# Which queue issues the loads of queries and residual tokens in the fused attention and routing stage

## The chip, the core and the metric

The kernel runs on one core of a Trainium2 chip. A core has TensorE (PE, matmuls), VectorE (DVE), ScalarE (ACT), GpSimd (POOL) and SyncE (SP), each with its own instruction stream, and 16 DMA engines that move data between SBUF and HBM. SyncE and ScalarE each have a hardware queue for DMAs (q1 and q10 in the trace), GpSimd a software queue (q0). The streams meet at semaphores. The metric is the device time of one execution in microseconds, lower is better.

## The reference

For x of 4 sequences of 2048 tokens with 512 channels the reference computes one layer:

```
x = x + layernorm(attention(layernorm(x)))          # linear attention with random features, 16 heads of 32
x = x + layernorm(ffn(layernorm(x)))                # 32 experts, top 4 of each token, plus a shared expert

attention: q_phi, k_phi = sorf_phi(rope(q)), sorf_phi(rope(k))      # exp of 128 features a head
           S, sum_k = sum over l of k_phi v,  sum over l of k_phi
           out = (q_phi S) / max(q_phi sum_k, EPS)                  # numerator over denominator, for each head and token
           return out @ w_out.T
```

The denominator is one number for a head and a token. It is what travels through DRAM below.

## The kernel before

The 8192 tokens are cut into NG = 16 groups of G = 512, each into A = 4 tiles of 128. A first stage normalises x, stores it centred (`xc`), projects it to queries, keys and values and stores the queries (`qk`, `norm`); a second sums the keys' features. The stage of this case is the third, `attend_and_route_programs` (line 782). Five programs, one for each engine, run over STEPS steps; in step s each engine does its part for several tiles at different distances behind, written out by hand. `group_at(s, lag)` says which group, if any, is due in step s with that lag. After the stage the same engines go on with the expert stage.

In step s TensorE makes the logits of quarter s+1 of the queries (L891, a quarter is 4 heads of a group), the numerators and denominators of quarter s (L901, L910), projects tile s-8 (L922), and turns and gates an earlier tile (L934, L948). ScalarE makes the features from the logits (`make_phi`, L991, twice a step, and the logits' place is free for TensorE only then), squares, copies the numerators to `heads` (L999), copies turned tiles (L1030) and makes the high half of normalised tiles (L1021). VectorE adds, measures and makes the low halves, and chooses experts.

Once a group, the denominators make a round trip. With n the group:

- VectorE, step 4(n+1): `read_total` (L1109) writes `den`.
- SyncE: `spread_share(n)` (from L855) stores it with four DMAs (L860), waits, loads it back with 64 tokens on each of 128 partitions as `dens` (L862).
- VectorE, step 4(n+1)+1: `make_share` (L1116) inverts it.
- SyncE stores `share` (L864), waits, and loads it with four broadcast DMAs into `spread`, 1 MB in SBUF (L869).
- VectorE, step 4n+6: `divide` (L1121), `heads` times `spread`. Its next instructions stand behind it. ScalarE, in the same step, waits for it in `make_at_high` (L1005), then goes on; VectorE makes the low half (L1125), and TensorE can project the group.

SyncE's queue carries, besides, the loads of a group's queries (`load_q`, by `load_heads`, lines 79 to 86: three DMAs of 512 KB and one of 32 KB, L82 and L84), into two buffers of which one is `keep["ahead"]`, and of the centred tokens that are added back (`load_x`, L852, 1 MB). Its order is a loop: queries of n+1, the round trip of n-1, the tokens of n-1. ScalarE's queue carries three stores of 1 MB a group: `x1` after `make_at_high` (L1042, step 4n+14 for group n), `rows` (L1047, step 4n+16) and the turned tiles (L1052, step 4n+17). GpSimd makes the reciprocal roots and scatters slots (L1261).

Of the kernel before, what the change touches and what calls it, by code (L numbers as in the profile page):

```python
# [5 lines left out]
P = 128  # L6
# [7 lines left out]
G = 512  # L14
NG = T // G
A = G // P
EC = E // P
# [764 lines left out]
def attend_and_route_programs(nc, io, keep, t):  # L782

    with ExitStack() as tiles:
        t.ctx = tiles
        PHIS, XS = 4, 3
# [4 lines left out]
        qT = [keep["ahead"], t.sb("qT1", [KR, H, G], F16)]  # L791
# [6 lines left out]
        x = [t.sb(f"x{r}", [P, A, E]) for r in range(XS)]  # L798
# [22 lines left out]
        x_loaded, x_stored = ([t.sem(f"{n}{r}") for r in range(XS)] for n in ("x_loaded", "x_stored"))  # L821
# [16 lines left out]
        def group_at(s, lag):  # L838

            return (s - lag) // A if s >= lag and (s - lag) % A == 0 and (s - lag) // A < NG else None  # L840

        def sp_program(sp):
            def load_q(n):
                if n >= 2:
                    sp.wait_ge(logits_ready, 2 * EC * (n - 1))
                load_heads(sp, io, qT[n % 2], n, 0, q_loaded[n % 2])

            def load_x(n):
                if n >= XS:
                    sp.wait_ge(x_low_ready, A * (n - XS + 1))  # L850
                    sp.wait_ge(x_stored[n % XS], 16 * (n // XS))
                sp.dma_start(x[n % XS][:], io["xc"][n * G:(n + 1) * G, :].rearrange("(a p) e -> p a e", p=P)  # L852
                             ).then_inc(x_loaded[n % XS], 16)

            def spread_share(n):  # L855
                sp.wait_ge(den_ready, n + 1)
                if n >= 1:
                    sp.wait_ge(share_ready, n)
                for i in range(HPC):
                    sp.dma_start(io["den"][n, i], den[D * i:D * i + EC, :]).then_inc(den_stored, 16)  # L860
                sp.wait_ge(den_stored, 16 * HPC * (n + 1))
                sp.dma_start(dens[:], io["den"][n].rearrange("i c (k q) -> (i c k) q", q=KP)).then_inc(dens_loaded, 16)  # L862
                sp.wait_ge(share_ready, n + 1)
                sp.dma_start(io["share"][n].rearrange("i c (k q) -> (i c k) q", q=KP), share[:]).then_inc(share_stored, 16)  # L864
                sp.wait_ge(share_stored, 16 * (n + 1))
                if n >= 1:
                    sp.wait_ge(at_ready, n)
                for i in range(HPC):
                    sp.dma_start(spread[D * i:D * i + D].rearrange("p c n -> p (c n)"),  # L869
                                 io["share"][n, i:i + 1].rearrange("o c n -> o (c n)").to_broadcast([D, EC * G])  # L870
                                 ).then_inc(spread_loaded, 16)

            load_q(1)
            for n in range(1, NG + 1):
                if n + 1 < NG:
                    load_q(n + 1)
                spread_share(n - 1)
                load_x(n - 1)

        def pe_program(pe):  # L880
            def make_logits(q, b):
# [101 lines left out]
                    count(n)  # L983

        def act_program(act):
            def make_phi(q, b):
                m = 2 * q + b
                act.wait_ge(logits_ready, m + 1)
                if q >= 2:
                    act.wait_ge(total_ready, q - 1)  # L990
                nc.scalar.activation(phi[m % PHIS][:].rearrange("p h q -> p (h q)"), logits[:], ACT.Exp,  # L991
                                     scale=1.0 / M_SCALE).then_inc(phi_ready, 1)

            def read_numer(q):
                n, c = q // EC, q % EC
                act.wait_ge(numer_ready, q + 1)
                if n >= 2:
                    act.wait_ge(at_low_ready, n - 1)
                nc.scalar.activation(heads[n % 2][:, c, :], numer[:], ACT.Copy).then_inc(numer_read, 1)  # L999

            def make_at_high(n):
                act.wait_ge(at_ready, n + 1)
                if n >= 2:
                    act.wait_ge(y_ready, A * (n - 1))
                nc.scalar.activation(at_hl[n % 2][:, 0], heads[n % 2][:], ACT.Copy).then_inc(at_high_ready, 1)  # L1005

            def square(m):
                k = m % 2
                act.wait_ge(y_ready, m + 1)
                if m >= 2:  # L1010
                    act.wait_ge(var_ready, m - 1)
                nc.scalar.activation(squares[k][:], y[k][:], ACT.Square, scale=E ** -0.5,
                                     accum_out=mv[k][:, 0, 1:2]).then_inc(y_squared, 1)

            def make_high(m):
                n, a, k = m // A, m % A, (m + 1) % 2
                act.wait_ge(rstd_ready, m + 2)
                if a == 0 and n >= 2:
                    act.wait_ge(rows_stored[n % 2], 16 * (n // 2))
                    act.wait_ge(turned_ready, A * (n - 1))  # L1020
                nc.scalar.activation(hl[n % 2][:, a, 0, :], x[n % XS][:, a, :], ACT.Copy,  # L1021
                                     scale=rstd[k][:, 1:2]).then_inc(x_high_ready, 1)

            def copy_turned(m):
                n, a = m // A, m % A
                act.wait_ge(turned_ready, m + 1)
                if a == 0 and n >= 2:
                    act.wait_ge(gates_ready, n - 1)
                    act.wait_ge(xT_stored[n % 2], 16 * (n // 2))
                nc.scalar.activation(xT[n % 2][:, :, :, a * P:(a + 1) * P],  # L1030
                                     turned[:].bitcast(F16).rearrange("p (s c q) -> p s c q", s=2, c=EC),
                                     ACT.Copy).then_inc(xT_ready, 1)

            def make_score(n):
                act.wait_ge(gates_ready, n + 1)
                if n >= 1:
                    act.wait_ge(slots_ready, n)
                nc.scalar.activation(grown[:].rearrange("p a e -> p (a e)"), gates, ACT.Exp, scale=-1.0).then_inc(score_ready, 1)

            def store_x1(n):  # L1040
                act.wait_ge(x1_ready, A * (n + 1))
                act.dma_start(io["x1"][n * G:(n + 1) * G, :].rearrange("(a p) e -> p a e", p=P),  # L1042
                              x[n % XS][:]).then_inc(x_stored[n % XS], 16)

            def store_rows(n):
                act.wait_ge(x_low_ready, A * (n + 1))
                act.dma_start(io["rows"][n * G:(n + 1) * G, :].rearrange("(a p) n -> p a n", p=P),  # L1047
                              hl[n % 2][:].rearrange("p a s e -> p a (s e)")).then_inc(rows_stored[n % 2], 16)

            def store_turned(n):  # L1050
                act.wait_ge(xT_ready, A * (n + 1))
                act.dma_start(io["xT2"][n], xT[n % 2][:].rearrange("p s c q -> p (s c q)")).then_inc(xT_stored[n % 2], 16)  # L1052

            for b in range(2):
                make_phi(0, b)
            for s in range(STEPS):
                n = group_at(s, SCORE)
                if n is not None:
                    make_score(n)
                if s + 1 < NT:  # L1060
                    make_phi(s + 1, 0)
                if 0 <= s - SQUARE < NT:
                    square(s - SQUARE)
                if s < NT:
                    read_numer(s)
                if s + 1 < NT:
                    make_phi(s + 1, 1)
                if 0 <= s - COPY < NT:
                    copy_turned(s - COPY)
                if 0 <= s - SPLIT < NT:  # L1070
                    make_high(s - SPLIT)
                n = group_at(s, A + 2)
                if n is not None:
                    make_at_high(n)
                n = group_at(s, A - 1 + ADD + 1)
                if n is not None:
                    store_x1(n)
                n = group_at(s, A - 1 + TURN + 1)
                if n is not None:
                    store_rows(n)  # L1080
                n = group_at(s, A - 1 + COPY + 1)
                if n is not None:
                    store_turned(n)
            for k in range(2):
                act.wait_ge(xT_stored[k], 16 * NG // 2)
                act.wait_ge(rows_stored[k], 16 * NG // 2)
            for r in range(XS):
                act.wait_ge(x_stored[r], 16 * ((NG - 1 - r) // XS + 1))
# [790 lines left out]
```

## Time and profile before

| | |
|---|---|
| runs | 2131.26 us median of 3 (2128.41 to 2144.04) |
| profiled execution | 2139.98 us; 2138.2 from its first to its last instruction |
| PE busy | 1843.4 us, 86% of the span |
| DVE busy | 1183.8 us, 55% |
| ACT busy | 1071.0 us, 50% |
| POOL busy | 756.9 us, 35% |
| mean granted clock of TensorE | 0.939 of full |
| q1 (SyncE) | 239.19 MB, 38.1% of the 16 DMA engines' time |
| q10 (ScalarE) | 124.26 MB, 16.5% |
| the stage of this case | about 866 to 1410 us of the span |

A row of an engine's timeline gives the start in microseconds, the duration, the engine, the line, the operation and what it writes and reads; in brackets stands the idle time before it and what ended it. `SPq` and `ACTq` are DMA issues on SyncE's and ScalarE's queues: their duration is that of the issue, not of the transfer. A busy PE is not PE at its peak, and idle time of an engine that sets nothing costs nothing.

### The profile page before, as it was taken

To read this page: it belongs to the slowest core of one execution; us is meant where nothing else is said; L and a number is where in the kernel's file an instruction comes from. 1 tells how busy PE (TensorE), PEld (TensorE's weight loads), DVE (VectorE), ACT (ScalarE), POOL (GpSimd) and SP (SyncE) were. 2 spreads that over 40 slices of the span, in tenths; PEclk is the share of its full clock that TensorE was granted. 3 is DMA by queue.
4 is the path that set the end of the run, shared out by engine and by line. 5 is a ranking of instruction groups with operands and counts; after the bars stand their busy time and mean duration, and the time that the engine had idled before them with its cause. 6 is when DMAs were issued, how large, how long until landed. Compare 5 with 4: busy or idle time off the path is not lost.

```text
span 2138.2 us, 33516 instructions
## 1 busy us (share of the span) xinstructions
PE 1843.4 (86%) x12976; PEld 892.7 (42%) x12976; DVE 1183.8 (55%) x2055; ACT 1071.0 (50%) x1371; POOL 756.9 (35%) x716
## 2 busy tenths in 40 slices
PE   8899999999988999699789888635998999987785
PEld 6444444444436888133233333322444444443231
DVE  7676766666650000156778878762444444445786
ACT  5555554545524666566566666412444444432443
POOL 0000000000000000013578787875677777761110
PEclk9999999999998999899899999867999999998897
DMA  6636354454527888567887785443799999987983
GB/s 231 232 124 239 132 193 178 168 203 165 178 103 209 211 212 205 120 175 188 225 221 239 220 235 183 161 183 100 169 197 221 247 241 246 205 146 241 334 288 126
DMA packets 197295, 421.92 MB, mean 197 GB/s; under 512 B 34068, under 2 KB 72340, under 8 KB 180512
## 3 DMA queue, kind: packets, MB, share of 16 engines
q1 hardware_dynamic: 91632, 239.19, 38.1%
q10 hardware_dynamic: 68640, 124.26, 16.5%
q0 software_dynamic: 36864, 56.32, 14.2%
q8 instruction: 103, 1.69, 0.3%
q14 instruction: 56, 0.46, 0.1%
HBM read 237.06 MB, written 193.86 MB: 202 GB/s over the span
## 4 chain that ended last, share of the span: by engine, by line
DMA 16%; PE 11%; DVE 10%; issue 9%; POOL 7%; ACT 3%; SPq 1%; POOLq 0%; DVEq 0%; ACTq 0%
DMA acc_dram<-s_y,s_slot 6%; DMA s_spread<-share_dram 5%; POOL acc_dram L1427 3%; PE s_gates L1486 2%; PE s_y L922 2%; PE s_ups L1486 2%; POOL slot_dram L1261 2%; DMA share_dram<-s_share 2%; DVE s_heads L1121 2%; PE s_ys L1501 1%; DMA s_dens<-den_dram 1%; DMA den_dram<-s_den 1%; DVE s_stats L1652 1%; DVE s_x L1675 1%; PE s_logits L891 1%
## 5 line engine op out<-in xcount | busy, mean ns | idle before, releaser
L271 PE MATMUL s_proj<-s_xT,keep_wqkv 128*128 128x512 f16 x1536 | 343.5, 380 | 0.0
L1261 POOL DMA_INDIRECT slot_dram<-keep_filled,keep_slots x256 | 274.1, 1071 | 76.2 <-issue 73.5
L1427 POOL DMA_INDIRECT acc_dram<-s_y,s_slot x128 | 204.5, 1597 | 92.7 <-issue 36.2
L271 PEld LDWEIGHTS s_proj<-s_xT,keep_wqkv 128*128 128x128 f16 x1536 | 148.2, 98 | 184.5 <-issue 14.8
L922 PE MATMUL s_y<-keep_wo,s_at_hl 128*128 128x512 f16 x768 | 197.2, 412 | 19.2 <-DVE s_x L1133 19.0
L250 PE MATMUL s_proj<-keep_wqkv,s_xT 128*128 128x512 f16 x768 | 181.4, 395 | 32.4 <-ACT s_xT L524 32.4
L1541 ACT ACTIVATE s_gate<-s_gates 128x512 f32<-128x512 f32 x96 | 57.1, 597 | 264.6 <-PE s_ups L1486 223.6
L1611 DVE SCALAR_TENSOR_TENSOR s_h<-s_gate,s_ups 128x512 f32<-128x512 f32 x96 | 65.9, 686 | 215.0 <-ACT s_gate L1541 215.0
L542 ACT ACTIVATE s_hl<-s_rot 128x1024 f16<-128x1024 f32 x64 | 67.6, 1057 | 231.3 <-DVE s_rot L413 230.5
L991 ACT ACTIVATE s_phi<-s_logits 128x1024 f32<-128x1024 f32 x128 | 131.5, 1027 | 99.2 <-PE s_logits L891 98.4
L400 DVE TENSOR_TENSOR s_by_cos<-s_proj,s_table 128x1024 f32<-128x1024 f32 x64 | 78.3, 1224 | 185.5 <-PE s_proj L271 184.4
L352 POOL TENSOR_SCALAR s_rstd<-s_mv 128x4 f32<-128x4 f32 x16 | 3.7, 229 | 499.7 <-DVE s_mv L367 499.7
L700 ACT ACTIVATE s_phi<-s_logits 128x1024 f32<-128x1024 f32 x128 | 131.1, 1024 | 86.9 <-PE s_logits L721 86.9
L1413 POOL DMA_INDIRECT s_rows<-rows_dram,s_slot x128 | 133.1, 1040 | 42.9 <-issue 32.0
L1532 ACT ACTIVATE s_xT<-s_turned 128x1024 f16<-128x1024 f16 x128 | 125.5, 1019 | 41.4 <-PE s_turned L1463 41.4
L922 PEld LDWEIGHTS s_y<-keep_wo,s_at_hl 128*128 128x128 f16 x768 | 74.7, 104 | 161.8 <-issue 72.2
L761 PE MATMUL s_parts<-s_phi,s_v 128*33 128x128 f32 x2048 | 138.7, 278 | 3.7 <-DMA s_v<-v_dram 3.6
L1501 PE MATMUL s_ys<-s_w,s_parts 128*128 128x512 bf16 x512 | 131.0, 379 | 3.5 <-DVE s_y L1628 3.5
L1486 PE MATMUL s_gates<-s_xT,s_w 128*128 128x512 f16 x512 | 124.5, 387 | 10.3 <-ACT s_xT L1532 10.3
L250 PEld LDWEIGHTS s_proj<-keep_wqkv,s_xT 128*128 128x128 f16 x768 | 75.8, 101 | 130.8 <-ACT s_xT L524 39.6
L1486 PE MATMUL s_ups<-s_xT,s_w 128*128 128x512 f16 x512 | 121.6, 380 | 0.0
L1628 DVE TENSOR_SCALAR s_y<-s_ys,s_slot 128x512 f32<-128x512 f32 x128 | 93.9, 748 | 42.0 <-PE s_ys L1501 41.5
(166 smaller groups left out, 3154.9 us busy)
## 6 DMA issues: line engine op xcount, KB each, us to landing
qk_dram<-s_hl ACTq DMA_DIRECT2D x32, 1024.0 KB
keep_ahead<-qk_dram SPq DMA_DIRECT2D x48, 512.0 KB
acc_dram<-s_zero SPq DMA_DIRECT2D x17, 1024.0 KB, 13.1
v_dram<-s_v ACTq DMA_DIRECT2D x16, 1056.0 KB
s_v<-v_dram SPq DMA_DIRECT2D x16, 1056.0 KB
s_x<-x_in SPq DMA_DIRECT2D x16, 1024.0 KB
xc_dram<-s_x SPq DMA_DIRECT2D x16, 1024.0 KB
s_spread<-share_dram SPq DMA_DIRECT2D x64, 256.0 KB
```

The source lines that it names most:

```text
L250: mm = nc.tensor.matmul(proj[half][:, 512 * b:512 * b + 512], left, right, start=(c == 0 and i == 0), stop=(c == EC - 1 and i == 2))
L271: mm = nc.tensor.matmul(out[:, 512 * b:512 * b + 512], left, right, start=(c == 0 and i == 0), stop=(c == EC - 1 and i == 2))
L700: nc.scalar.activation(phi[n % 2][:].rearrange("p h m -> p (h m)"), logits[n % 2][:], ACT.Exp, scale=1.0 / M_SCALE).then_inc(phi_ready, 1)
L761: mm = nc.tensor.matmul(parts[ch % 2][at:at + D + 1, h // 2 * M:(h // 2 + 1) * M], v[n % 2][:, a * H + h, :], phi[half][:, h % HALF, :], s ...
L922: mm = nc.tensor.matmul(y[m % 2][:], at_hl[n % 2][:, s, c, a * P:(a + 1) * P], keep["wo"][:, w, c, :], start=(c == 0 and i == 0), stop=(c ...
L991: nc.scalar.activation(phi[m % PHIS][:].rearrange("p h q -> p (h q)"), logits[:], ACT.Exp, scale=1.0 / M_SCALE).then_inc(phi_ready, 1)
L1261: nc.gpsimd.indirect_dma_start(out=io["slot"], out_offset=bass.IndirectOffsetOnAxis(ap=slots[n % 2][:, a * K + j:a * K + j + 1], axis=0), ...
L1413: nc.gpsimd.indirect_dma_start(out=rows[r][:, a, :], out_offset=None, in_=io["rows"], in_offset=bass.IndirectOffsetOnAxis(ap=slot[e % RING ...
L1427: nc.gpsimd.indirect_dma_start(out=io["acc"], out_offset=bass.IndirectOffsetOnAxis(ap=slot[e % RING][:, a, 0:1], axis=0), in_=y[e % 2][:, ...
L1486: mm = nc.tensor.matmul(bank[:], w[:, c, i * P:(i + 1) * P], left[:, s, c, :], start=(c == 0 and s == 0), stop=(c == EC - 1 and s == 1))
L1501: mm = nc.tensor.matmul(ys[a % 2][:], parts[p % 2][:, i, s, a * P:(a + 1) * P], w[:, i, :], start=(i == 0 and s == 0), stop=(i == IC - 1 a ...
L1532: nc.scalar.activation(xT[k][:, :, :, a * P:(a + 1) * P], turned[a % 2][:].bitcast(F16).rearrange("p (s c q) -> p s c q", s=2, c=EC), ACT. ...
```

## The change

`load_q` and `load_x` move, with their waits, from SyncE's program to ScalarE's. ScalarE issues the queries of group n+2 at the end of its step 4(n+1), after `make_high` and ahead of the rows store of the same step, and the tokens of group n in step 4n+6, right after `make_at_high` and ahead of the x1 store of the same step. SyncE keeps the queries of group 1, before the loop, and the round trip of each group. Nothing of the arithmetic, the buffers or the transfers' shapes changes.

```diff
         def sp_program(sp):
-            def load_q(n):
-                if n >= 2:
-                    sp.wait_ge(logits_ready, 2 * EC * (n - 1))
-                load_heads(sp, io, qT[n % 2], n, 0, q_loaded[n % 2])
-
-            def load_x(n):
-                if n >= XS:
-                    sp.wait_ge(x_low_ready, A * (n - XS + 1))
-                    sp.wait_ge(x_stored[n % XS], 16 * (n // XS))
-                sp.dma_start(x[n % XS][:], io["xc"][n * G:(n + 1) * G, :].rearrange("(a p) e -> p a e", p=P)
-                             ).then_inc(x_loaded[n % XS], 16)
-
...
-            load_q(1)
-            for n in range(1, NG + 1):
-                if n + 1 < NG:
-                    load_q(n + 1)
-                spread_share(n - 1)
-                load_x(n - 1)
+            load_heads(sp, io, qT[1], 1, 0, q_loaded[1])
+            for n in range(NG):
+                spread_share(n)
...
         def act_program(act):
+            def load_q(n):
+                if n >= 2:
+                    act.wait_ge(logits_ready, 2 * EC * (n - 1))
+                load_heads(act, io, qT[n % 2], n, 0, q_loaded[n % 2])
+
+            def load_x(n):
+                if n >= XS:
+                    act.wait_ge(x_low_ready, A * (n - XS + 1))
+                    act.wait_ge(x_stored[n % XS], 16 * (n // XS))
+                act.dma_start(x[n % XS][:], io["xc"][n * G:(n + 1) * G, :].rearrange("(a p) e -> p a e", p=P)
+                             ).then_inc(x_loaded[n % XS], 16)
+
...
                 if 0 <= s - SPLIT < NT:
                     make_high(s - SPLIT)
+                n = group_at(s, A)
+                if n is not None and n + 2 < NG:
+                    load_q(n + 2)
                 n = group_at(s, A + 2)
                 if n is not None:
                     make_at_high(n)
+                    load_x(n)
                 n = group_at(s, A - 1 + ADD + 1)
                 if n is not None:
                     store_x1(n)
```

## Rows read from the trace of the kernel before

**Rows 1.** Busy time by stretch, nine groups: window, PE, PEld, DVE, ACT, POOL, clock, DMA, GB/s.
```profile
1061.90:1335.20 273.30, 244.97 (x1851) 90.64 (x1850) 216.79 (x497) 179.96 (x268) 210.83 (x217) 0.95 0.77 222
```
**Rows 2.** Waits of VectorE in the same stretch: us in total, times, longest.
```profile
DVE s_heads L1121 <- DMA s_spread<-share_dram: 31.3, 9, 4.1
```
**Rows 3.** Timeline of SyncE's queue, group 7: start, us, what.
```profile
1092.46 1.27 SPq L860 DMA_DIRECT2D den_dram<-s_den  x4
1095.89 0.34 SPq L862 DMA_DIRECT2D s_dens<-den_dram  x1
...
1104.78 3.32 SPq L869 DMA_DIRECT2D s_spread<-share_dram  x4
...
1111.01 1.25 SPq L82 DMA_DIRECT2D keep_ahead<-qk_dram  x3
```
**Rows 4.** Timelines of ScalarE and VectorE, group 7.
```profile
1098.04 0.37 ACTq L1047 DMA_DIRECT2D rows_dram<-s_hl  x1
...
1102.36 0.28 ACT L1038 ACTIVATE s_grown<-s_route 128x128 f32<-128x128 f32 x1 [1.52 <-issue]
...
1104.67 0.35 ACTq L1052 DMA_DIRECT2D xT_dram<-s_xT  x1
...
1116.35 0.37 ACTq L1042 DMA_DIRECT2D x_dram<-s_x  x1
...
1102.20 0.54 DVE L1116 RECIPROCAL s_share<-s_dens 128x64 f32<-128x64 f32 x1
...
1114.02 2.29 DVE L1121 TENSOR_TENSOR s_heads<-s_heads,s_spread 128x2048 f32<-128x2048 f32 x1 [3.52 <-DMA s_spread<-share_dram]
```
**Rows 5.** The rows store and the divide of group 6, timelines.
```profile
1065.26 0.37 ACTq L1047 DMA_DIRECT2D rows_dram<-s_hl  x1
...
1082.75 2.29 DVE L1121 TENSOR_TENSOR s_heads<-s_heads,s_spread 128x2048 f32<-128x2048 f32 x1 [3.33 <-DMA s_spread<-share_dram]
```
**Rows 6.** DMA queues (packets, MB, share) in 1117.5:1122.5, 1122.6:1125.6, 389.9:392.9; two issues.
```profile
q1 hardware_dynamic: 159, 1.04, 99.1%
...
q10 hardware_dynamic: 451, 0.92, 86.7%
...
q10 hardware_dynamic: 856, 0.88, 100.4%
...
383.34 1.03 ACTq L562 DMA_DIRECT2D qk_dram<-s_hl  x2
...
388.69 0.37 SPq L169 DMA_DIRECT2D s_x<-x_in  x1
```
**Rows 7.** DMA queues in 1115.8:1122.5 (queries), 1099:1102 (rows store), 1105:1109.4 (turned store).
```profile
q1 hardware_dynamic: 220, 1.47, 102.9%
...
q10 hardware_dynamic: 521, 1.03, 88.8%
...
q10 hardware_dynamic: 128, 1.05, 72.6%
```
**Rows 8.** Group 1's round trip on SyncE's queue and VectorE, timelines.
```profile
914.57 0.35 SPq L862 DMA_DIRECT2D s_dens<-den_dram  x1
...
918.39 1.71 SPq L869 DMA_DIRECT2D s_spread<-share_dram  x4
...
916.33 0.55 DVE L1116 RECIPROCAL s_share<-s_dens 128x64 f32<-128x64 f32 x1 [4.52 <-DMA s_dens<-den_dram]
...
924.90 2.29 DVE L1121 TENSOR_TENSOR s_heads<-s_heads,s_spread 128x2048 f32<-128x2048 f32 x1 [2.12 <-DMA s_spread<-share_dram]
```
**Rows 9.** Busy time by stretch after three divides, columns as in rows 1.
```profile
1085.10:1098.00 12.90, 9.92 (x54) 3.01 (x58) 12.26 (x27) 8.11 (x12) 10.01 (x10) 0.74 0.69 177
1206.80:1218.40 11.60, 8.63 (x54) 2.80 (x58) 11.12 (x23) 8.01 (x12) 7.67 (x7) 0.85 0.85 211
...
1116.30:1126.40 10.10, 7.85 (x62) 2.63 (x58) 9.75 (x20) 8.09 (x12) 6.59 (x6) 1.00 0.95 239
```
**Rows 10.** VectorE's divide of group 4, timeline.
```profile
1021.97 2.29 DVE L1121 TENSOR_TENSOR s_heads<-s_heads,s_spread 128x2048 f32<-128x2048 f32 x1 [13.82 <-DMA s_spread<-share_dram]
```

## The prediction

> **What bounds the kernel now.** I read the page first, for the shares of the engines, then the waits of the fused stage, then the instructions of one group of tokens on SyncE, ScalarE and VectorE, then which DMA queue moved bytes in chosen stretches. I call a group by its number n, and R is the moment at which ScalarE's queue issues that group's `rows_dram` store (step 4(n+1)): all times of a group are counted from R, because the change puts the loads of queries just ahead of that very instruction.
>
> The stage keeps TensorE, VectorE and ScalarE busy and moves 222 GB/s with the 16 DMA engines busy 0.77 of the time [rows 1]: there is room for about 7 us of stalls in a group of 30.4 us (273.3 us for nine groups), no more. Where the engines stop is one place. VectorE sits idle before `divide` until the load of `spread` has landed, 31.3 us in nine groups [rows 2]. ScalarE's next instruction needs the quotient and waits with it; ScalarE also reads the logits, so TensorE stops behind both. That wait is at the end of the denominators' round trip, and nothing hides it: each microsecond that the spread lands later is a microsecond on all engines.
>
> Group 7 shows the round trip [rows 3, 4]. Its denominators are stored at 1092.46, loaded back transposed at 1095.89, inverted by VectorE at 1102.20 (0.54 us), then stored, and the spread is issued at 1104.78; `divide` starts at 1114.02. With R = 1098.04 the share is inverted at R+4.2, stored from R+4.7, the spread is issued at R+6.7 and used at R+16.0. The share does not wait for the DMA: the denominators are back in time, and VectorE reaches that instruction only then. Over the nine groups 6 to 14 the use of the spread lies between R+15.9 and R+17.5; group 6, the longest, is shown [rows 5]; the mean of the nine is 16.6.
>
> **In what order the DMA engines work.** This decides the case. In group 7 the x1 store is issued on ScalarE's queue (q10) at 1116.35 [rows 4], 4 us after the last load of queries on SyncE's queue (q1). From 1117.5 to 1122.5 the two hardware queues move 159 packets on q1 and none on q10; from 1122.6 to 1125.6 q10 moves 451. The same the other way round in the first stage: q10 gets two stores of 1 MB at 383.34, q1 a load at 388.69; from 389.9 to 392.9 q10 moves 856 packets and q1 none [rows 6]. So a transfer on one queue waits for everything that the other queue was given earlier, whichever direction it goes and however many transfers that is. A queue of its own gives a transfer no way past the others: who was issued first goes first.
>
> **What the change does, part by part.**
>
> *Taken from SyncE.* Its waits for logits and for `x` go. They cost nothing: the loads are issued at 1111.01 in group 7 [rows 3], and the next denominators are due a period of 30.4 us after 1092.46, at about 1123; SyncE has 12 us to spare. Gain 0. What cover there was is the long idle time of that queue.
>
> *Added to ScalarE.* Per group four issues for the queries (three take 1.25 us on SyncE [rows 3], so four at most 1.7) and one for x, 0.4 by the same rate. ScalarE's sequencer issues DMAs while its earlier activations still run: `rows_dram` is issued at 1098.04, and the step's next instruction that needs the engine's attention is `grown` at 1102.36 [rows 4]. 1.7 us fit in these 4.3. Were they to take twice as long, as four spread issues did (3.32 us [rows 3] against 1.71 in group 1 [rows 8]), they still fit; and what is lost between R and the divide is taken off the wait at the divide. Below: 0. Above: 1.7 us in the few groups with no wait, under 5 us in all. I take 0. The wait of `load_q` for `logits_ready` is met two steps earlier by the order of ScalarE's own work, and `load_x` needs semaphores of a group before; behind them are only the two stores and the next step's activations. Queries are issued some 20 us after today's moment and still 3 steps ahead of their use; x 4 steps ahead. Neither becomes late: 0.
>
> *Moved in time: the load of queries.* Today it goes behind the spread, at R+13 [rows 3], where only the x1 store waits for it. After, it goes at R, ahead of the rows store, ahead of the share's store (R+4.7), ahead of the turned store (R+6.6) and of the spread. The bytes are the same, but they now stand before the round trip. Sizes: the load of queries moves 1.47 MB in 6.7 us, so 1.57 MB in 7.1; the rows store 1.03 MB in under 3.0, I take 2.6; the turned store's 128 packets are in a stretch of 4.4 us of which 72.6% are its own, 3.2 us, less its start, 2.7 [rows 7]. The spread takes 6.5 us from issue to use in group 1, with the engines free [rows 8]; 0.9 of that is the start, and what is left, 5.6, I put at 5.9 beside GpSimd's scatters: 4.3 on the engines, 1.6 until `divide`.
>
> Sum by order of issue: R + 0.9 (issue to first packet: the rows store of 1098.04 moves in the stretch from 1099 on) + 7.1 (queries) + 2.6 (rows) + 0.3 (share) + 2.7 (turned store; it was issued before the spread can be) + 4.3 (spread) + 1.6 (last packet to `divide`) = R+19.5. The spread is issued at about R+12.5, inside the time of the turned store, so that the queue and not the round trip's latency sets it. Against 16.6: **2.9 us** more per group, all of it in a place where the wait already lasts 3.5 us, so nothing is absorbed. For groups 4 to 13, ten of them: **29 us**. Groups 14 and 15 have no load of queries ahead: 0.
>
> *Groups 0 to 3*, where the steps are shorter and there are no rows or turned stores. In group 1 the denominators are loaded back at 914.57, inverted at 916.33, used at 924.90 [rows 8]. The load of queries will be issued about a microsecond ahead of 914.57 and hold the engines until 921.5; the inversion follows at 923, **6.7 us** late, and so does the divide. By the same steps groups 0, 2 and 3 lose 4.2, 3.9 and 2.8. Sum **17.6 us**.
>
> *The clock.* From ScalarE's release after the divide to the next R, TensorE had the full clock (1.00, 2.4 GHz) in group 7 and took 10.1 us; after group 6, whose stall was as long as others, it had 0.74 (half clock for part) and took 12.9 [rows 9]. The usual case between is 11.6 us at 0.85. With the wait at the divide at 6.4 us instead of 3.5 I expect the 12.9 as the rule: **1.3 us** per group more, ten groups, **13 us**. Below 0 (the stretch stays at 11.6), above 2.8 (all come from 10.1).
>
> Sum: 29 + 17.6 + 13 = **60 us**. The profiled execution took 2138.2 us between first and last instruction, 2139.98 with what lies around it. It holds one disturbance: in group 4 `divide` waited 13.8 us [rows 10], 10 more than in any near it, which the mean above leaves out; without it the execution is at 2130, as the median of the runs, 2131.3. So I add to the median: 2131 + 60 = **2191 us**. Nothing later takes it back: GpSimd's scatters and the next stage start from the last groups' routing, which shifts with the divides.
>
> **Rivals.**
> *The load back falls behind the queries.* In group 7 it is issued 2.15 us before R, but where TensorE ran at full clock R comes sooner and the two collide. Then the denominators return at R+12.3, the share is stored behind the turned store, and the divide is at about R+21.2: 4.6 instead of 2.9. 46 + 17.6 + 13 = 77, with a longer half clock some 2215 us. For it: group 1 does just that. Against: a longer wait before means a slower stretch to R.
>
> *The queues share.* Each engine alternates between the two queues. Then the share's store is hardly held, the spread is issued at R+6.7, finds 5.6 us of q10's work left, and ends after twice its own 4.3: R+7.7+8.6+1.6 = R+17.9, 1.3 late; 13 + half of the 17.6 = 22, **2153 us**. For it: where both queues are given work within a tenth of a microsecond, as the turned store and the spread of group 7 at 1104.67 and 1104.78, the stretch that follows holds both. Against: both pairs of stretches where one queue waited behind the other [rows 6]. The Trainium skill, page "DMA: Bandwidth & Descriptors", section "Queues, rings and completion order", says that each engine goes round-robin over the queue rows with work, a packet at a time. It would make this rival the forecast; the trace does not agree where one queue's work was given earlier.
>
> *The other side: the lone queue is prompt.* If q1 passes what waits on q10, the spread is used 2.06 + 6.5 us after the inversion, as in early groups, at R+12.8; the wait of 3.5 us goes in 12 groups (42 us), and the half clock with it (13 us): **2076 us**. It decides as soon as the spread starts ahead of the turned store. Against: the load on q1 that waited behind q10's stores [rows 6]. The same page, section "Issuing engines are not separate DMA queues", says that several issuing engines save only the issue time; that too gives this rival nothing.
>
> *Hidden anyway.* The loads moved cost and gain less than 1%: it would need the engines to finish 7.1 us of queries before the share is stored at R+4.7. Against: 7.1 is more than 4.7.
>
> **Numbers.** First-issued-first 0.62 (2191; its own range 2165 to 2205), load back late 0.13 (2215), sharing 0.12 (2153), prompt 0.07 (2076), hidden 0.06 (2131). The range leaves out the last two and a tail above: 2148 to 2222. One per cent is 21 us, about what a measurement of this kernel can tell from no change. Slower by over 1%: 0.62 + 0.13 + most of 0.12 = 0.83; within: 0.10; faster: 0.07.
>
> **What would show it.** In the changed kernel: q10 alone busy from R+1 to about R+10.5; from the share's store to the spread's issue 7 us instead of 2; `divide` at R+19 to R+20 in groups 4 to 13 and idle time before it of 6 us instead of 3.5; TensorE's half clock longer after each. Groups 14 and 15 as before. I am wrong if the share's store lands within 2 us while q10 holds the queries, or if the divide stays at R+16.5; wrong in size if the load back is what comes late.

## The result and the profile after

The changed kernel takes 2220.99 us (median of 4 runs, 2220.68 to 2221.37) against 2132.96 for the kernel before (4 runs): ratio 1.0398, 95% interval 1.0369 to 1.0427, 88 us slower. The forecast was 2191 us, range 2148 to 2222. The range holds it by one microsecond. In the two profiled executions the spans are 2218.9 and 2138.2 us; the accounts below add up to that difference, 80.7 us.

Busy time by stretch, eight groups (6 to 13, from the reading of one total to that of the eighth next), of the kernel before; columns as in [rows 1].

```profile
1061.90:1304.70 242.80, 217.75 (x1645) 80.04 (x1644) 192.75 (x441) 161.60 (x240) 187.74 (x193) 0.95 0.79 228
```

The same eight groups of the changed kernel, and the stretch from the divide of group 6 to the issue of the queries in group 7:

```profile
1092.90:1387.10 294.20, 222.93 (x1651) 80.51 (x1650) 192.47 (x441) 162.22 (x240) 176.71 (x193) 0.87 0.72 191
1121.50:1135.70 14.20, 8.84 (x54) 2.82 (x58) 13.65 (x25) 8.20 (x12) 5.93 (x5) 0.68 0.54 154
```

The work is the same (VectorE 192.75 and 192.47 us busy), the eight groups are 51.4 us longer. The waits of VectorE say where; first before, then after (us in total, times, longest):

```profile
DVE s_heads L1121 <- DMA s_spread<-share_dram: 27.4, 8, 4.1
```
```profile
DVE s_heads L1122 <- DMA s_spread<-share_dram: 76.4, 8, 11.2
```

49.0 of the 51.4 us are this one wait, the one of [rows 2]. R is again the start of the instruction that stands at the end of ScalarE's step 4(n+1): in the kernel before the rows store, in the changed one the first issue of the queries. Group 7 in the changed kernel, SyncE's queue, then ScalarE and its queue, then VectorE, to be read against [rows 3, 4]:

```profile
1131.24 1.26 SPq L848 DMA_DIRECT2D den_dram<-s_den  x4
1133.83 0.34 SPq L850 DMA_DIRECT2D s_dens<-den_dram  x1
1140.39 0.34 SPq L852 DMA_DIRECT2D share_dram<-s_share  x1
1149.00 2.16 SPq L857 DMA_DIRECT2D s_spread<-share_dram  x4
...
1135.67 0.33 ACTq L82 DMA_DIRECT2D s_qT<-qk_dram  x1
...
1137.61 0.38 ACTq L1044 DMA_DIRECT2D rows_dram<-s_hl  x1
...
1139.99 0.28 ACT L1035 ACTIVATE s_grown<-s_route 128x128 f32<-128x128 f32 x1 [1.53 <-PE s_route L933]
...
1142.29 0.35 ACTq L1049 DMA_DIRECT2D xT_dram<-s_xT  x1
...
1139.82 0.54 DVE L1117 RECIPROCAL s_share<-s_dens 128x64 f32<-128x64 f32 x1
...
1159.02 2.29 DVE L1122 TENSOR_TENSOR s_heads<-s_heads,s_spread 128x2048 f32<-128x2048 f32 x1 [10.90 <-DMA s_spread<-share_dram]
```

In group 7 R is 1135.67. Up to the inversion nothing is late (R+4.15, as before). Then the share's store, 32 KB on a queue that carries nothing else, is issued at 1140.39 and the spread can be issued only at 1149.00: 8.6 us where it was about 2. The divide is at R+23.4 instead of R+16.0. What the DMA queues moved in three stretches shows why (packets, MB, share of the 16 engines' time): 1136.7 to 1144.6, 1144.6 to 1150, and 1150 to 1157.5.

```profile
q10 hardware_dynamic: 214, 1.49, 99.6%
q14 instruction: 1, 0.01, 0.5%
q0 software_dynamic: 32, 0.00, 0.3%
...
q10 hardware_dynamic: 620, 1.66, 97.1%
q1 hardware_dynamic: 144, 0.03, 2.9%
...
q1 hardware_dynamic: 189, 1.04, 64.2%
q10 hardware_dynamic: 82, 0.53, 23.8%
```

In the first stretch the store of the share has been waiting for 4 us and q1 moves no packet at all: the engines work on the queries, which q10 was given first. The share's packets come in the second stretch, the spread in the third, behind what is left of the turned store. The order of issue is coarse, though. The share does not wait for the last packet of the rows store, issued 2.8 us before it: between 1145.5 and 1147.5 the 144 packets of q1 go through beside 329 of q10, and from 1147.5 to 1150 q10 moves another 228. It is the same in the groups around.

The means of the eight groups say which half of the way is longer. From the issue of the share's store to that of the spread it is 8.3 us, where it was 1.8; from the issue of the spread to the divide 9.4 us, where it was 9.5. The whole loss is the time for which the share's store is held.

### The profile page after: what moved, and what is told of

It is laid out like the page before. It is cut to its first block, busy times and chain, and to the rows that moved or that the text cites. A ratio compares the mean times of both kernels' runs of the same rounds, so it can differ in the third digit from the quotient of the medians.

```text
span 2218.9 us, 33516 instructions
## 1 busy us (share of the span) xinstructions
PE 1854.9 (84%) x12976; PEld 894.1 (40%) x12976; DVE 1182.1 (53%) x2055; ACT 1070.0 (48%) x1371; POOL 741.6 (33%) x716
## 4 chain that ended last, share of the span: by engine, by line
DMA 16%; PE 15%; DVE 9%; issue 8%; POOL 6%; ACT 5%; SPq 1%; ACTq 1%; POOLq 0%; DVEq 0%
DMA s_spread<-share_dram 5%; DMA share_dram<-s_share 5%; PE s_gates L1487 3%; DMA acc_dram<-s_y,s_slot 3%; PE s_ups L1487 3%; PE s_y L907 2%; PE s_ys L1502 2%; POOL slot_dram L1262 2%; DMA s_rows<-rows_dram,s_slot 2%; POOL acc_dram L1428 2%; DVE s_heads L1122 2%; ACT s_xT L1533 1%; ACT s_phi L988 1%; PE s_total L895 1%; PE s_logits L876 1%
## 5 line engine op out<-in xcount | busy, mean ns | idle before, releaser
L1262 POOL DMA_INDIRECT slot_dram<-keep_filled,keep_slots x256 | 263.7, 1030 | 79.0 <-issue 77.1
L907 PEld LDWEIGHTS s_y<-keep_wo,s_at_hl 128*128 128x128 f16 x768 | 74.4, 104 | 165.7 <-issue 80.7
L1253 POOL TENSOR_TENSOR s_rstd<-s_mv,s_eps 128x2 f32<-128x2 f32 x65 | 41.1, 633 | 241.1 <-ACT s_squares L1009 120.5
## 6 DMA issues: line engine op xcount, KB each, us to landing
acc_dram<-s_zero SPq DMA_DIRECT2D x17, 1024.0 KB, 13.8
```

The source lines that it names most:

```text
L907: mm = nc.tensor.matmul(y[m % 2][:], at_hl[n % 2][:, s, c, a * P:(a + 1) * P], keep["wo"][:, w, c, :], start=(c == 0 and i == 0), stop=(c ...
L1262: nc.gpsimd.indirect_dma_start(out=io["slot"], out_offset=bass.IndirectOffsetOnAxis(ap=slots[n % 2][:, a * K + j:a * K + j + 1], axis=0), ...
```

## Experiments

Two theories for the 88 us. **A**: the two hardware queues are served in the order of issue, so it is the moment at which the queries are issued that costs. **B**: it is ScalarE's queue or stream that costs, as it now issues five more DMAs a group.

**Only x moved.** `load_q` stays in SyncE's loop, `load_x` is in ScalarE's program as in the change.

```diff
-            load_heads(sp, io, qT[1], 1, 0, q_loaded[1])
-            for n in range(NG):
-                spread_share(n)
+            load_q(1)
+            for n in range(1, NG + 1):
+                if n + 1 < NG:
+                    load_q(n + 1)
+                spread_share(n - 1)
```

> One part of the change alone: the load of x is issued on ScalarE's queue after make_at_high, the loads of queries stay on SyncE's queue where they were. Theory A (what is issued first on either hardware queue is served first, so only the moment of the queries' loads counts): x now stands behind the spread's use, where nothing of the round trip waits, so 2131 us, between 2120 and 2140, and the wait before divide stays at about 3.5 us in groups 6 to 14. Theory B (issuing on ScalarE's queue itself costs, one instruction of five moved): a fifth of the 88 us, about 2149 us.

Measured: 2137.21 us against 2131.77, ratio 1.0021 (0.9997 to 1.0045). The wait of eight groups:

```profile
DVE s_heads L1121 <- DMA s_spread<-share_dram: 27.8, 8, 4.4
```

As before. The move of x costs nothing that these runs can tell (the interval ends at 10 us), and the wait is the queries'.

**Queries on SyncE's queue, at the early moment.** ScalarE issues none of them.

```diff
 # spread_share, after the load back of the denominators
+                if n + 2 < NG:
+                    load_q(n + 2)
                 sp.wait_ge(share_ready, n + 1)
```

> The queries back on SyncE's queue, but early: SyncE issues those of group n+2 between the load back of the denominators and the store of the share, about 1.5 us before the moment at which the changed kernel issues them on ScalarE's queue. ScalarE keeps only the load of x. Theory A: as slow as the changed kernel less the 1.5 us in ten groups, 2195 to 2221 us, wait before divide 8 to 10 us. Theory B: ScalarE is relieved, so 2131 to 2140 us.

Measured: 2197.95 us, ratio 1.0307 (1.0256 to 1.0358). SyncE's queue in group 7 (start, us), and the divide:

```profile
1123.50 0.34 SPq L855 DMA_DIRECT2D s_dens<-den_dram  x1
1123.89 1.79 SPq L82 DMA_DIRECT2D s_qT<-qk_dram  x3
1125.72 0.29 SPq L84 DMA_DIRECT2D s_qT<-norm_dram  x1
1129.91 0.34 SPq L859 DMA_DIRECT2D share_dram<-s_share  x1
1136.30 2.11 SPq L864 DMA_DIRECT2D s_spread<-share_dram  x4
...
1145.34 2.29 DVE L1121 TENSOR_TENSOR s_heads<-s_heads,s_spread 128x2048 f32<-128x2048 f32 x1 [7.70 <-DMA s_spread<-share_dram]
```

ScalarE is relieved, and the kernel still loses 66 of the 88 us. From the queries' issue to the divide it is 21.5 us here and 23.4 in the changed kernel in group 7, but 22.0 and 22.4 in the mean of groups 6 to 13. The queries are issued 0.4 us behind the load back here and 2.1 us there: 1.7 us a group earlier, so 17 of the 23 us between the two kernels in ten groups. B falls as the cause; some 6 us are left that B could still claim.

**A third of the bytes.** The changed kernel with two of the three large transfers of the queries cut to a sixteenth; it leaves out that part of the input.

```diff
+        k = H // 2 * G if r == 0 else G // 2
...
-                     io["qk"][n, s, which].rearrange("i (d h) n -> d i (h n)", d=D)).then_inc(loaded, 16)
+                     io["qk"][n, s, which].rearrange("i (d h) n -> d i (h n)", d=D)[:, :, 0:k]).then_inc(loaded, 16)
```

> The changed kernel with the same number of issues at the same place, but of the three 512 KB transfers of a group's queries two are cut to a sixteenth (from group 2 on, so the logits are computed from stale rows: this part of the input is left out). Theory A: the queries hold the engines 3 us instead of 8, divide moves from R+22.6 to R+17.5, 50 us less in ten groups and some 10 in the first ones: 2150 to 2170 us. Theory B: the issues are the same, so 2215 to 2221 us.

Measured: 2154.23 us, ratio 1.0100 (1.0051 to 1.0149); the wait of eight groups is 35.7 us where it was 76.4. With as many issues, 67 of the 88 us are gone. It is the bytes in front, not the issues.

**Both loads on ScalarE's queue, the queries after the divide.** If only the front of the spread counted, this would be as fast as before.

```diff
-                n = group_at(s, A)
-                if n is not None and n + 2 < NG:
-                    load_q(n + 2)
...
                     make_at_high(n)
                     load_x(n)
+                    if n + 3 < NG:
+                        load_q(n + 3)
```

> Both loads on ScalarE's queue as in the changed kernel, but the queries of group n+3 are issued in step 4n+6, after make_at_high and the load of x, instead of those of n+2 in step 4(n+1): the moment at which SyncE issued them before. Theory A: the round trip has no queries in front of it, divide comes back to R+16 to R+17 and the time to 2125 to 2145 us. Theory B (ScalarE's queue or its stream pays for the issues): as the changed kernel, 2215 us.

Measured: 2174.19 us, ratio 1.0197 (1.0145 to 1.0249): neither. Its waits in eight groups:

```profile
DVE s_share L1118 <- DMA s_dens<-den_dram: 26.6, 8, 5.4
DVE s_heads L1123 <- DMA s_spread<-share_dram: 20.1, 8, 3.6
```

The wait before the divide is smaller than in the kernel before, but a new one stands before the inversion. I had called this SyncE's old moment, and it isn't: SyncE issued the queries while the spread was still on its way [rows 3], 3 us before the divide; here they come 2 us after it, behind x and ahead of the x1 store. Of these 3.7 MB the queries are still in the engines when the next denominators are stored: in group 8 that store is issued at 1141.11, q1 moves no packet before 1146, and the load back is issued at 1148.16, 7 us after the store, where it was 3.4 us in [rows 3], and behind a rows store of 1146.61. It is the same order of issue, met at the round trip's first half. Here too it is coarse: the denominators' packets move beside those of the x1 store, which was issued 4.8 us before them.

**The turned store moved**, as a test of what else stands in front of the spread: on the changed kernel one step later; on the kernel before one step later, and one step earlier. Each is one line, `group_at(s, A - 1 + COPY + 1)` with `+ 2` or without `+ 1`.

> The changed kernel with the store of the turned tiles moved one step later, out of the round trip; the queries still stand in front. Theory A: 3 us less before the divide in ten groups, as x, x1 and turned store (9.4 us) are just done when the next denominators come: 2180 to 2200 us, wait before divide 7 us instead of 10. If the turned store did not matter: 2221 us.

> The kernel before with only the store of the turned tiles moved one step later, to after make_at_high of the next group due, so that it no longer stands in front of the spread. Theory A (served in the order of issue): the spread is used 2.5 us earlier, near R+14, but x, queries, x1 and turned store, 17 us of the engines, are now all issued between R+10 and R+17 and the next denominators are stored about 25 us after R: their load back becomes late, as in the run with the queries after the divide. Net between 2105 and 2135 us, with a wait of VectorE for the denominators of 2 to 5 us a group. If only the place ahead of the spread counted: 2100 us.

> The kernel before with only the store of the turned tiles moved one step earlier, right behind the rows store of the same step at R, so that both are through the engines by R+6.5, when the spread is issued. Theory A: the share's store waits about 1.5 us, the spread has the engines to itself and is used near R+14.5 instead of R+16.6; 2 us in eleven groups and some half clock with it: 2095 to 2115 us. If the order of issue did not matter: 2131 us.

Measured: 2191.05 (ratio 1.0303, 1.0262 to 1.0345), 2121.73 (0.9971, 0.9956 to 0.9986) and 2123.39 us (0.9979, 0.9963 to 0.9994). The waits of eight groups, in this order:

```profile
DVE s_share L1117 <- DMA s_dens<-den_dram: 53.4, 8, 8.0
DVE s_heads L1122 <- DMA s_spread<-share_dram: 9.9, 8, 2.9
```
```profile
DVE s_share L1116 <- DMA s_dens<-den_dram: 14.8, 7, 4.0
DVE s_heads L1121 <- DMA s_spread<-share_dram: 10.7, 8, 2.7
```
```profile
DVE s_heads L1121 <- DMA s_spread<-share_dram: 17.8, 8, 4.3
...
DVE s_share L1116 <- DMA s_dens<-den_dram: 8.9, 5, 2.6
```

All as A has it in kind: what leaves the front of the spread shortens that wait and, when it goes behind the divide, comes back before the inversion. In size two of the three were off. On the changed kernel the time was as expected, but not its place: 7 us a group were to be left before the divide, and it is 1.2 there and 6.7 before the inversion. On the kernel before the move is worth little, 0.2 to 0.3% by ratios whose intervals exclude 1, and the earlier one less than expected (2095 to 2115). These two are the only complete kernels here that beat the kernel before, and by next to nothing.

**A third of the queries early, two thirds behind the spread**, on the kernel before, alone and with the turned store later.

```diff
-                load_heads(sp, io, qT[n % 2], n, 0, q_loaded[n % 2])
+                load_part(sp, io, qT[n % 2], n, 0, q_loaded[n % 2], (1, 2, 3) if n >= 3 else (0, 1, 2, 3))
...
+                if n >= 1 and n + 2 < NG:
+                    load_part(sp, io, qT[n % 2], n + 2, 0, q_loaded[n % 2], (0,))
                 sp.wait_ge(share_ready, n + 1)
```

> The kernel before with one of a group's four query transfers (512 KB, rows 0 to 31 of the tile) taken out of the load behind the spread and issued on SyncE's queue right after the denominators are loaded back, about 2 us before R; the other three stay behind the spread. Theory A (served in the order of issue, and there is a gap of some 7 us of engine time between the load back and the share's store, of which the rows store takes 3): a third fits in the gap, the share's store is held by at most 1 us and the x1 store is through 2.7 us sooner: 2120 to 2135 us. If any query bytes ahead of the share cost their own time: a third of the 66 us that the full load cost there, 2153 us.

> As the run with a third early, and the store of the turned tiles one step later, behind the divide. Theory A: in front of the spread there is no turned store, and behind the divide 2.7 us less than in the run with the turned store later alone, so the next denominators' load back is late by 1 us instead of 2 to 4: 2100 to 2115 us. If the gap does not hold the third: 2120 us or more.

Measured: 2136.60 (ratio 1.0032, 1.0013 to 1.0051) and 2127.84 us (1.0002, 0.9975 to 1.0030). A third in the gap costs 3 to 11 us by the interval, not a third of 66, which fits a gap that holds most of these bytes; that the gap is what decides was not tested otherwise. Both runs missed what was expected, the first by 2 us, the second by 13, at what had been named for a gap that does not hold the third (2120 or more). Against the run with the third alone the turned store's move gives 9 us, about what it gave without the third (7); it only pays for what the third costs.

**The first scatter.** In both profiles group 4's divide waits longer than that of group 5: 13.8 against 3.5 us before [rows 10], 19.4 against 11.9 after. The edit on the kernel before: `bounds_check=(0 if n == 0 else NSLOT - 1)`. It drops the writes of the first group's slots except slot 0, so the expert stage misses a part of its table.

> The kernel before with the scatter of the first group's slots reduced to those of slot 0 (left out: the writes of all other slots of group 0, so part of the routing table is missing and the expert stage reads less). In every trace so far group 4's divide waits 10 us longer than its neighbours, while GpSimd scatters the first group's slots. If those writes slow the other transfers, group 4's wait falls from 13.8 to about 3.5 us and the time by up to 10 us, to 2121; if it is something else that happens at that moment, the wait stays.

Measured: 2122.71 us against 2128.49, ratio 0.9977 (0.9961 to 0.9992). Group 4's divide:

```profile
1005.75 2.29 DVE L1121 TENSOR_TENSOR s_heads<-s_heads,s_spread 128x2048 f32<-128x2048 f32 x1 [3.40 <-DMA s_spread<-share_dram]
```

The 10 us of this wait are gone, and the median falls by 6. A shorter expert stage is not the reason: from the last divide to the end of the span it is 782.8 us here and 782.9 before.

## Why the prediction held, and where its steps were off

The mechanism is the one that was forecast. The number is in the range with some luck: it lies 16 us above what was given for this mechanism alone (2165 to 2205), and nearest to the 2215 of a rival, the late load back, that did not happen. Of the 60 us, 29 for the wait were less than half of what was measured, and 13 for the clock made up for a part of that.

**The order of the engines' work: held.** It was read from two pairs of stretches of the kernel before [rows 6], and the changed kernel shows it in the 4 us in which the share's store waits and q1 moves nothing. It is coarser than the prediction had it: the share waits for the queries, but moves beside the rows store. As a forecast the sharing rival is out by that stretch, and so is the Trainium skill's rule of a round of the queue rows ("DMA: Bandwidth & Descriptors", "Queues, rings and completion order") as a description of how the queries and the share's store meet; packets of both queues side by side, as that rule would have them, show only once the rows store is under way. The prompt rival fell with it. The same page's other rule, in "Issuing engines are not separate DMA queues", that several issuing engines save only issue time, is what the runs show: counted from the issue, the divide comes after 22.0 us with the queries on SyncE's queue and after 22.4 on ScalarE's.

**Issues on ScalarE, 0: held.** The four issues and the rows store run from 1135.67 to 1137.99 beside activations, and `grown` starts 4.3 us after R, as before. **x, 0: held** by its own run, to within its interval.

**The load back late: did not happen** after group 1. In group 7 it is issued 1.8 us before R, and the inversion has no wait in the eight groups.

**Groups 0 to 3, 17.6 us: the sum held by luck, its parts did not.** The divide of group 3 is at 998.17, in the kernel before at 980.46, 17.7 us late. In group 1 the load back waits behind the queries as worked out (against [rows 8]):

```profile
916.07 0.34 SPq L850 DMA_DIRECT2D s_dens<-den_dram  x1
...
921.32 0.55 DVE L1117 RECIPROCAL s_share<-s_dens 128x64 f32<-128x64 f32 x1 [7.67 <-DMA s_dens<-den_dram]
...
933.10 2.29 DVE L1122 TENSOR_TENSOR s_heads<-s_heads,s_spread 128x2048 f32<-128x2048 f32 x1 [8.24 <-DMA s_spread<-share_dram]
```

Group 1 lost 6.4 us (8.2 late at 933.10, of which group 0 had brought 1.9) where 6.7 was forecast; groups 0, 2 and 3 lost 1.9, 6.0 and 3.5, against 4.2, 3.9 and 2.8.

**2.9 us per group: the term that was mis-sized.** The wait grew by 49.0 us in eight groups, 6.1 each. The mean of the divide in groups 6 to 13 went from R+16.6 to R+22.4. Between the two issues the sum had it nearly right: it let the share's store go at R+4.7 and the spread at R+12.5, 7.8 us, and 8.3 were measured. The step that failed is the overlap behind it. The sum gave the spread 7.0 us from its issue to the divide, 2.5 less than in the kernel before, because the turned store was to run while the share was still on its way. The measured 9.4 us are those of the kernel before: in group 7, when the spread is issued at 1149.00, q10 has 0.86 MB still to move, most of the turned store.

The whole chain was slower than the sum had it, too. The sum set each transfer at the rate of a stretch in which the engines were full [rows 7]: 4.8 MB in 17.0 us, 282 GB/s. In group 7 they took from about 1136.7 to 1157.5, 20.8 us, 231 GB/s. Piece by piece: the first 7.9 us moved 1.49 MB, 189 GB/s, where the queries behind the spread had moved 1.47 in 6.7 us; at R+14.3, when by my sum the turned store was through for 0.7 us, 0.53 MB of q10 and the whole spread were still to come, and took 7.5 us. SyncE waits for all of the share's store before it issues the spread, and a transfer is through only when the last of the 16 engines is; that this makes the chain longer than bytes over rate is only argued, the sizes are measured. In the run with a third of the query bytes the wait is 4.5 us a group (35.7 in eight), 1.0 more than before.

**The clock, 13 us: wrong.** TensorE did get the half clock for longer: 0.68 in the stretch from the divide to the next R, 0.87 over eight groups instead of 0.95. The stretch from a divide to the next R is longer, 14.4 us in the mean where it was 13.7, but the groups are not longer by it. What VectorE needs in a group besides the wait at the divide is (294.2 - 76.4) / 8 = 27.2 us, where it was (242.8 - 27.4) / 8 = 26.9: 0.3 us a group, 3 in ten instead of 13. VectorE is busy for 13.65 of the 14.20 us in that stretch, so there VectorE sets the pace, and TensorE at the lower clock keeps up. The three rows of [rows 9] say the same: VectorE is busy for 12.26 of 12.90 us, 11.12 of 11.60 and 9.75 of 10.10. The 12.9 us were read as TensorE's doing, and are more work of VectorE (27 instructions against 20).

**The base: wrong by some 10 us in the account, harmless in the sum.** I took group 4's long wait for a disturbance of that execution. It is in every trace here with the first group's scatter (group 4 waits 3 to 16 us longer than group 5), and it goes when that scatter is left out. So the profiled execution had no 10 us to give back, and it stands above the median only as one run among others.

The groups of the profile add up: 17.7 us to group 3, 64.7 in groups 4 to 13 (forecast 29 + 13), where the waits at the divide alone grew by 62.9, and -1.6 in groups 14 and 15, where no queries stand in front (group 14's rows store is at 1391.97 and its divide at 1408.38, R+16.4, wait 3.95). 80.8 of 80.7.

**Open.** Why the turned store's move to an earlier step gave 5 us instead of 15 or more on the kernel before: the divide came between R+14.8 and R+18.5 in groups 5 to 14, where R+14.5 was expected; part of the difference is back in the wait before the inversion (8.9 us in eight groups, 2.6 before), the rest is not traced. What slows the queries when they are the first of a chain. And why a small transfer waits for the transfers ahead of the running one, and then moves beside the running one.

## What to carry to other kernels

Another engine's DMA queue doesn't take a transfer out of anybody's way: in these traces the two hardware queues of a core are one line, and its order is, roughly, the order of issue. So when loads are moved to another queue, draw the line of transfers in time and look at what small, awaited store or load now stands behind the moved bytes; give bulk the gaps in which no round trip is open, as far as it fits in them (none of the moves tried here gained more than 0.3%). Size such a chain by transfers that were measured from issue to use, not by bytes over the full rate.

## What was not expected of the hardware

Scatters of the first group's slots, 16 DMAs of 128 rows of 8 bytes, slowed the transfers beside them: group 4's wait is 13.8 us with them and 3.4 without. Two transfers show it, each by about 5 us. The share's store of 32 KB took 6.9 us to the issue of the spread, 1.5 without them, and the turned store's packets went from 1003 to 1011 where they took 3.5 us without. The scatters of later groups, as many, did no such thing; why the first did was not tested. And ScalarE's sequencer issued five DMAs in 2.3 us beside running activations, and `grown`, the next instruction behind them, started 4.3 us after R with them as without.
